# A transformer block on one core: loads by need and own orders in the opening, and the causal mask by blocks of 32

## The chip, the core and the metric

The kernel runs on one core of a Trainium2 chip. The metric is the device time of one execution in microseconds. A core has a matrix engine (TensorE, PE in the profile; its weight loads are PEld), VectorE (DVE), ScalarE (ACT), GpSimd (POOL) and SyncE (SP), which here only issues DMAs. They run side by side and wait for each other by semaphores.

## The reference

16 sequences of 256 tokens, width 256. Attention with an adapter ahead of it, then a conditional layer and a gated FFN, each with a residual:

```python
h = relu(x @ W1[lang] + b1); u = x + h @ W2[lang] + b2     # adapter by language
n = layernorm(u) * gamma[lang] + beta[lang]
q = (n @ Wq.T) as 16 heads of 16; k = n @ Wk.T; v = n @ Wv.T   # one key/value head
mask = (q_pos >= k_pos)                                    # 256 tokens: the window of 256 hides nothing
probs = softmax(where(mask, q k / 4, -1e30)); x = x + (probs v) @ Wf.T + bf
y = gelu(x @ fc1.T + b); y = [y @ fc2.T + b | y @ experts[id].T + b]
h = silu(y w1) * (y w2); h = gelu(h h1); h = gelu(h h2)    # each with its scales
x = x + (h w3) * s3
```

The whole runs in float32; the big products are taken as sums of fp32r parts.

## The kernel before

The program is written by hand for each engine, with the instructions of an engine in the order of its code. There is no scheduler: every order that matters is written out in the functions `iteration` of each engine, in `all_iterations`, and in the straight code ahead of it.

Attention works in a pipeline over the 16 batches. Iteration b does four things at once: the front of batch b + 2 (adapter, normalisation, projections of queries and keys), the maxima of batch b + 1, the scores and exponentials of batch b, and the tail of batch b - 1 (probabilities times values, output projection, residual). Iteration -1 and iteration 0 (which have no tail, and -1 no scores) stand ahead of a hardware loop over iterations 1 to 12, and 13 to 15 behind it.

Queries and keys of a batch lie in one of three slots of `q_t` and `keys`. A slot of 64 rows per parity of heads holds the high and low parts of 16 query channels (rows 0 to 47) and two rows for the negated maximum (48 and 49); rows 50 to 63 were zero. SP moves the queries into the slot with six DMAs (`move_queries`, L321), and the maxima with four (`move_maxima`, L330).

The maxima of a batch take 12 units. `max_scores` (L1282, L1285) computes the scores of two or four heads for one tile of 128 queries into one of two banks, 512 columns of float32 in all, and adds the causal mask to the 128x128 diagonal blocks by a bf16 matmul of the identity with a mask of -1e30: 512 columns in the four units of the first query tile, 256 in the eight of the second. VectorE takes the maxima (L927), splits them (L941, L943), TensorE transposes them (L1290), ScalarE copies them out. `scores` (L1301) then computes the scores with the maximum subtracted, ScalarE the exponentials (L624), and GpSimd sets what lies above the diagonal to zero (L521).

In the opening SP issues all constant loads one after another and GpSimd clears `q_t` and the values; TensorE runs nine matmuls on zeros (L1484, `keep_warm`) while the first loads are under way. `load_front` loads the input and adapter of a batch in five DMAs: three that wait for the adapter matmuls of the batch ahead (`load_inputs`, L293 to L295) and two that wait for its normalisation (`load_rest`, L301, L302). After the moves of batch 2, SP loads the first two chunks of the hidden layers' weights (L414, L415) and copies the FFN weights from their input tensor to a scratch tensor in memory in one DMA (L338); `load_ffn` loads them from there at the end of the loop. TensorE's seven constant loads are counted by `const_loaded` (7 x 16 = 112), for which its transposes, ScalarE's first query copy and GpSimd's cast of the identity (L506) wait; the reciprocal root of the variance (L512) is GpSimd's as well, behind that cast.

## Time and profile before

| | us |
|---|---|
| median of 3 runs (1142.23 to 1147.89) | 1143.06 |
| the profiled execution | 1147.46 |
| its span | 1145.7 |
| TensorE busy (96%) | 1103.2 |
| VectorE busy (68%) | 783.1 |
| ScalarE busy (51%) | 589.5 |
| GpSimd busy (15%) | 173.4 |

### The profile page before, as it was taken

What the parts mean: (1) busy time and instruction counts of PE and PEld (TensorE: products, weight loads), DVE (VectorE), ACT (ScalarE), POOL (GpSimd) and SP (SyncE); (2) the same over time, 40 slices, a digit from 0 to 9 for tenths busy, and PEclk for the clock granted to TensorE, in tenths of its full rate; (3) what the DMA queues carried; (4) which work ended last, traced back from release to release, by engine and by line L of the source; (5) the groups of instructions that cost most, each with busy time, mean ns of one, the idle gap of its engine ahead of it and who ended that gap; (6) DMA issues with size and microseconds to landing.
All of it is one profiled execution on the core that took longest, in us unless ns stands there. A gap on an engine that the chain in (4) does not pass through costs nothing.

```text
span 1145.7 us, 17992 instructions
## 1 busy us (share of the span) xinstructions
PE 1103.2 (96%) x5947; PEld 869.3 (76%) x5963; DVE 783.1 (68%) x1377; ACT 589.5 (51%) x990; POOL 173.4 (15%) x192
## 2 busy tenths in 40 slices
PE   5697999999998999999999999999999999999998
PEld 3465777676765888888888888888888888888886
DVE  2565777777776567566487775777757787568875
ACT  1154656565656445434365654656545564455653
POOL 2021222222245443541000000000000000000000
PEclk9688999999999999999999999999999999999999
DMA  4455555546474456545414443144430444404421
GB/s 134 68 150 171 106 101 101 100 101 103 99 205 148 166 200 210 214 174 185 155 41 164 165 147 110 37 165 147 164 111 11 164 142 162 144 0 147 147 92 38
DMA packets 80591, 148.57 MB, mean 130 GB/s; under 512 B 15328, under 2 KB 41840, under 8 KB 80368
## 3 DMA queue, kind: packets, MB, share of 16 engines
q1 hardware_dynamic: 71026, 126.92, 38.8%
q10 hardware_dynamic: 9518, 21.11, 5.2%
q8 instruction: 19, 0.31, 0.1%
q14 instruction: 28, 0.23, 0.1%
HBM read 107.63 MB, written 30.41 MB: 120 GB/s over the span
## 4 chain that ended last, share of the span: by engine, by line
PE 91%; DVE 3%; DMA 1%; ACT 1%; SPq 1%; issue 1%; ACTq 0%; POOL 0%; DVEq 0%; POOLq 0%
PE bank L1599 35%; PE bank L1561 10%; PE bank L1364 7%; PE bank L1611 5%; PE bank L1282 4%; PE bank L1537 4%; PE bank L1531 4%; PE bank L1301 3%; PE bank L1248 3%; PE bank L1320 2%; PE bank L1356 2%; PE bank L1285 2%; PE bank L1218 2%; DMA vec<-in_cond_vec 1%; PE bank L1228 1%; PE bank L1258 1%
## 5 line engine op out<-in xcount | busy, mean ns | idle before, releaser
L1599 PE MATMUL bank<-op_hi,w_ring 128*128 128x512 f32 x896 | 348.7, 389 | 0.0
L1599 PE MATMUL bank<-op_lo,w_ring 128*128 128x512 f32 x896 | 348.6, 389 | 0.0
L1118 DVE TENSOR_TENSOR op_lo<-x_blk,op_hi 128x512 fp32r<-128x512 f32 x288 | 193.4, 683 | 30.4 <-ACT op_hi L805 30.3
L805 ACT ACTIVATE op_hi<-x_blk 128x512 fp32r<-128x512 f32 x288 | 162.8, 620 | 73.5 <-PE bank L1599 69.3
L1599 PEld LDWEIGHTS bank<-op_lo,w_ring 128*128 128x128 f32 x896 | 168.2, 188 | 35.0
L1599 PEld LDWEIGHTS bank<-op_hi,w_ring 128*128 128x128 f32 x896 | 168.1, 188 | 35.0
L927 DVE TENSOR_REDUCE neg_max<-bank 128x2 f32<-128x512 f32 (+1 forms) x192 | 124.8, 684 | 35.7 <-PE bank L1285 34.4
L624 ACT ACTIVATE p<-bank 128x512 f32<-128x512 f32 x192 | 108.7, 596 | 39.0 <-PE bank L1301 34.7
L829 ACT ACTIVATE x_blk<-x_blk,scales 128x512 f32<-128x512 f32 x96 | 69.3, 722 | 67.0 <-DVE x_blk L1171 28.9
L1561 PE MATMUL bank<-tile_hi,ffn_w 128*128 128x512 f32 x256 | 101.6, 397 | 0.0
L1561 PE MATMUL bank<-tile_lo,ffn_w 128*128 128x512 f32 x256 | 100.9, 394 | 0.0
L521 POOL TENSOR_SCALAR_AFFINE_SELECT p<-p 128x512 f32<-128x512 f32 (+1 forms) x96 | 75.9, 791 | 162.6 <-ACT p L624 162.5
L1301 PE MATMUL bank<-q_t,keys 128*128 128x512 f32 x192 | 94.0, 505 | 0.6 <-ACT p L624 0.6
L757 ACT ACTIVATE g_raw<-bank,fc_bias 128x512 f32<-128x512 f32 x64 | 44.0, 689 | 91.8 <-PE bank L1364 77.6
L1282 PE MATMUL bank<-keys,q_t 128*128 128x256 f32 (+1 forms) x256 | 85.9, 392 | 2.6 <-DVE neg_max L927 2.5
L817 ACT ACTIVATE sil<-bank,scales 128x512 f32<-128x512 f32 x64 | 43.9, 688 | 79.2 <-PE bank L1561 79.1
L1126 DVE SCALAR_TENSOR_TENSOR x_blk<-bank,scales,sil 128x512 f32<-128x512 f32 x64 | 48.1, 751 | 51.9 <-PE bank L1561 49.8
L1282 PEld LDWEIGHTS bank<-keys,q_t 128*128 128x128 f32 x256 | 49.7, 199 | 11.1 <-DVE neg_max L927 5.5
L562 POOL TENSOR_TENSOR comb<-comb 128x512 f32<-128x512 f32 x32 | 49.5, 1546 | 56.5 <-DVE g_parts L1084 55.0
L1561 PEld LDWEIGHTS bank<-tile_hi,ffn_w 128*128 128x128 f32 x256 | 48.1, 188 | 11.9
L1561 PEld LDWEIGHTS bank<-tile_lo,ffn_w 128*128 128x128 f32 x256 | 48.2, 188 | 11.2
L1285 PE MATMUL bank<-mask,ident_b 128*128 128x256 bf16 (+1 forms) x176 | 56.6, 322 | 0.0
(126 smaller groups left out, 1741.4 us busy)
## 6 DMA issues: line engine op xcount, KB each, us to landing
w_ring<-hid_scratch SPq DMA_DIRECT2D x112, 512.0 KB, 4.6
hid_scratch<-comb ACTq DMA_DIRECT2D x8, 1792.0 KB, 7.8
q_t<-q_high SPq DMA_DIRECT2D x64, 128.0 KB, 4.9
comb<-in_hid_d ACTq DMA_DIRECT2D x6, 768.0 KB, 5.1
xt<-in_x_t SPq DMA_DIRECT2D x16, 256.0 KB
xtok<-in_x_tok SPq DMA_DIRECT2D x16, 256.0 KB
resid<-in_x_t SPq DMA_DIRECT2D x16, 256.0 KB, 3.0
q_t<-q_rest SPq DMA_DIRECT2D x32, 128.0 KB, 4.6
```

The source lines that it names most:

```text
L521: nc.gpsimd.affine_select(out=v, in_=v, compare_op=ALU.is_ge, fill=0.0, base=0, pattern=[[0, v.shape[1]], [1, P]], channel_multiplier=-1). ...
L624: nc.scalar.activation(dst.rearrange("p c t -> p (c t)"), score_bank[par][:, :], ACT.Exp).then_inc(s["exp_done"], 1)
L805: nc.scalar.activation(op_hi[:, o % OP_RING, k], x_blk[:, operand_home(o), k], ACT.Copy).then_inc(s["op_hi"], 1)
L829: nc.scalar.activation(x_blk[:, at[block], m], src, ACT.Gelu, scale=sc[:, KB * row + m:KB * row + m + 1]).then_inc(s[made], 1)
L927: nc.vector.tensor_reduce(neg_max[:, t, first:first + pairs, :].rearrange("p c a -> p (c a)"), max_bank[u % 2][:, :].rearrange("p (c k) -> ...
L1118: nc.vector.tensor_tensor(op_lo[:, o % OP_RING, k], x_blk[:, operand_home(o), k], op_hi[:, o % OP_RING, k].bitcast(F32), ALU.subtract).the ...
L1282: mm(dst[:, 2 * c * seen:2 * (c + 1) * seen].rearrange("p (a k) -> p a k", a=2), q_t[slot][:, first + c, t * P:(t + 1) * P], keys[slot][:, ...
L1285: mm(diag, ident_b[:, :], mask[:, 0:2 * pairs, :], start=False, stop=True).then_inc(s["max_mm"], 1)
L1301: mm(score_bank[par][:, :].rearrange("p (c t) -> p c t", c=pairs), keys[slot][:, par, k0:k0 + P], q_t[slot][:, first:first + pairs, q0:T], ...
L1364: last = mm(bank, w[:, k, cols], v[:, k, :], start=i == 0, stop=i == len(passes) - 1)
L1561: last = mm(bank, w_at(at, k, HID, m), read(v[:, half, k, :]), start=k == 0 and v is yc_hi, stop=k == KD - 1 and v is yc_lo)
L1599: last = mm(banks[first_bank + m][:, :], w, read(v[:, q % OP_RING, k, :]), start=k == 0 and v is op_hi and i not in (P2, P3), stop=k == KB ...
```

## The change

There are two parts.

The causal mask. A table `rank_d` of 7 rows is loaded, rounded, and moved once into rows 50 to 56 of all three slots: for r = 1 to 7 the query row is 1 where the query's block of 32 is lower than r, and the key row is -1e30 where the key's block is r. Every product of queries and keys so carries the mask between blocks of 32. What is left is the triangle inside the blocks on the diagonal, and for it the mask matmul becomes four, each with 32 columns of the identity, for 32 query rows and their own 32 keys. ScalarE and VectorE write only rows 0 to 49 of the keys' slots now, and GpSimd clears the keys' slots as well.

The opening. The first adapter matmul waits for the input and the first adapter weight alone (`first_loaded`); the other constants are issued after these have landed, and wf only after the adapter inputs of batch 1. TensorE runs 10 matmuls on zeros at the start, 12 after the adapter of batch 0 and 12 after that of batch 1. Iterations -1 and 0 have orders of their own on PE, ACT and DVE. The first chunks of the hidden weights are loaded in iterations 10 and 11, and the copy of the FFN weights is cut into 12 pieces, one at the end of each loop iteration.

```diff
-WARM_LOADS, WARM_NORM = 9, 14
+WARM_LOADS, WARM_NORM, WARM_SECOND = 10, 12, 12
@@ sync
+            def move_ranks(slot):
+                sp.wait_ge(s["rank_made"], 1)
+                rows = slice(MASK_ROW, MASK_ROW + RANKS)
+                for to, part, count in ((q_t, 0, NP), (keys, 1, 2)):
+                    sp.dma_start(to[slot][rows, :, :].bitcast(F32),
+                                 rank[:, part, :].rearrange("p (c t) -> p c t", c=1).broadcast_to([RANKS, count, T])).then_inc(s["ranks_moved"], 16)
...
-            def store_ffn():
-                sp.dma_start(ffn_scratch[:, :], ffn_d).then_inc(s["ffn_copied"], 16)
+            def copy_ffn(i):
+                cols = bass.ds(i * FFN_PIECE, FFN_PIECE)
+                sp.dma_start(ffn_scratch[:, cols], ffn_d[:, cols]).then_inc(s["ffn_copied"], 16)
 
             def load_ffn():
-                sp.wait_ge(s["ffn_copied"], 16)
+                sp.wait_ge(s["ffn_copied"], 16 * FFN_PIECES)
...
-            sp.dma_start(wf[:, :, :], w_f).then_inc(s["const_loaded"], 16)
...
+            load_inputs(1, l)
+            sp.dma_start(wf[:, :, :], w_f).then_inc(s["const_loaded"], 16)
...
+            load_rest(1, l)
+            load_resid(0)
+            sp.wait_ge(s["const_made"], 7 + 2 * SLOTS)
+            for slot in range(SLOTS):
+                move_ranks(slot)
             move_queries(0, 0)
...
-            for c in range(2):
-                sp.dma_start(comb[c][:, A11:A11 + 3, :], hid_d[c, :, 0:3, :]).then_inc(comb_loaded[c % 2], 16)
-                sp.dma_start(comb[c][:, A21, :], hid_d[c, :, 3, :]).then_inc(comb_loaded[c % 2], 16)
-            store_ffn()
...
+                load_resid(b)
+                copy_ffn(b - 1)
...
+            for b in range(B - 3 - SLOTS, B - 3):
+                iteration(b, b % SLOTS)
+                if b < B - 4:
+                    load_first_chunk(b - (B - 3 - SLOTS))
@@ gpsimd: the clears of keys[0], keys[1], keys[2] beside those of q_t
+            nc.gpsimd.memset(keys[0][:, :, :].bitcast(F32), 0.0).then_inc(s["const_made"], 1)
@@ scalar
-                    nc.scalar.activation(keys[slot][:, par, :], kv[:, :], ACT.Identity,
+                    rows = slice(SLOT * par, SLOT * par + MASK_ROW)
+                    nc.scalar.activation(keys[slot][rows, par, :], kv[rows, :], ACT.Identity,
...
-            act.wait_ge(s["front_loaded"], 80)
+            act.wait_ge(s["front_loaded"], 48)
@@ vector
+            dve.wait_ge(s["rank_loaded"], 16)
+            nc.vector.tensor_copy(rank.bitcast(F32R), rank_raw).then_inc(s["rank_made"], 1)
@@ tensor
-                pe.wait_ge(s["front_loaded"], 80 * (n + 1))
+                if is_first(n):
+                    pe.wait_ge(s["first_loaded"], 32)
+                else:
+                    pe.wait_ge(s["front_loaded"], 80 * n + 48)
...
-                mm(diag, ident_b[:, :], mask[:, 0:2 * pairs, :], start=False, stop=True).then_inc(s["max_mm"], 1)
+                for at in range(0, P, BLOCK):
+                    own = slice(at, at + BLOCK)
+                    last = mm(diag[own, :, own], ident_b[:, own], mask[:, 0:2 * pairs, own], start=False, stop=True)
+                last.then_inc(s["max_mm"], 1)
```

On TensorE, in the loop, at the first two maximum units of an iteration (`bank<-keys,q_t` are the products of queries and keys, `bank<-mask,ident_b` the mask). Before:

```order
L1322 MATMUL bank<-p,values 32x128 x4
L1272 REGISTER_ALU
L1275 ISA [waits keys_out,q_moved]
L1282 MATMUL bank<-keys,q_t 128x256 [waits max_out]
L1282 MATMUL bank<-keys,q_t 128x256
L1285 MATMUL bank<-mask,ident_b 128x512
L1282 MATMUL bank<-keys,q_t 128x256 [waits max_t_out]
L1282 MATMUL bank<-keys,q_t 128x256
L1285 MATMUL bank<-mask,ident_b 128x512
L1329 REGISTER_ALU
L1340 MATMUL bank<-ident,pv 128x128 [waits hidden_out,late_out,early_out]
L1340 MATMUL bank<-ident,pv 128x128 x3
```

And now:

```order
L1415 MATMUL bank<-p,values 32x128 x4
L1360 REGISTER_ALU
L1365 ISA [waits keys_out,q_moved]
L1372 MATMUL bank<-keys,q_t 128x256 [waits max_out]
L1372 MATMUL bank<-keys,q_t 128x256
L1377 MATMUL bank<-mask,ident_b 32x4x32 x4
L1372 MATMUL bank<-keys,q_t 128x256 [waits max_t_out]
L1372 MATMUL bank<-keys,q_t 128x256
L1377 MATMUL bank<-mask,ident_b 32x4x32 x4
L1422 REGISTER_ALU
L1433 MATMUL bank<-ident,pv 128x128 [waits hidden_out,late_out,early_out]
L1433 MATMUL bank<-ident,pv 128x128 x3
```

Where one mask matmul of 512 columns stood there are four of 4 x 32 columns that write 32 rows each; the rest of the row is the same.

On TensorE in iteration -1, from the adapter of batch 1 (`bank<-xt,w1c`) on. Before:

```order
L1218 MATMUL bank<-xt,w1c 128x256
L1228 MATMUL bank<-w2c,h_t 128x256 [waits u_out,hidden_out]
L1228 MATMUL bank<-w2c,h_t 128x256
L1237 MATMUL bank<-ident,norm 128x128 [waits norm_ready]
L1237 MATMUL bank<-ident,norm 128x128 x3
L1248 MATMUL bank<-norm_t,wq 128x256 [waits q_low,norm_t_out]
L1248 MATMUL bank<-norm_t,wq 128x256 x3
L1282 MATMUL bank<-keys,q_t 128x256 [waits keys_out,q_moved]
L1282 MATMUL bank<-keys,q_t 128x256
L1285 MATMUL bank<-mask,ident_b 128x512
L1282 MATMUL bank<-keys,q_t 128x256 x2
L1285 MATMUL bank<-mask,ident_b 128x512
```

And now:

```order
L1304 MATMUL bank<-xt,w1c 128x256
L1316 MATMUL bank<-w2c,h_t 128x256 [waits u_out,hidden_out]
L1316 MATMUL bank<-w2c,h_t 128x256
L1293 MATMUL bank<-att 128x512 x12
L1325 MATMUL bank<-ident,norm 128x128 [waits norm_ready]
L1325 MATMUL bank<-ident,norm 128x128 x3
L1372 MATMUL bank<-keys,q_t 128x256 [waits ranks_moved,keys_out,q_moved]
L1372 MATMUL bank<-keys,q_t 128x256
L1377 MATMUL bank<-mask,ident_b 32x4x32 x4
L1372 MATMUL bank<-keys,q_t 128x256 x2
L1377 MATMUL bank<-mask,ident_b 32x4x32 x4
L1336 MATMUL bank<-norm_t,wq 128x256 [waits q_low,norm_t_out]
```

Twelve matmuls on zeros came in, and the first two maximum units of batch 0 stand ahead of the query projection of batch 1 (`bank<-norm_t,wq`) instead of behind it. They wait for the moves of the ranks too.

On SP in the opening, from the load of the key projection wkv on. Before:

```order
L393 DMA wkv<-in_w_kv 128x256
L394 DMA wf<-in_w_f 128x512
L395 DMA bf<-in_b_f 128x2
L396 DMA mask<-in_mask_d 128x512
L397 DMA key_row<-in_key_row_d 128x4
L312 DMA resid<-in_x_t 128x2x256
L400 DMA fc_raw<-in_fc_w 128x1024 x2
L401 DMA fc_bias<-in_fc_b 128x8
L402 DMA scales<-in_ffn_s 128x34
L289 TENSOR_LOAD in_lang_ptr
L289 REGISTER_ALU
L289 TENSOR_LOAD in_lang
```

And now (the register and load rows between are the read of a language id):

```order
L413 DMA mask<-in_mask_d 128x512
L414 DMA key_row<-in_key_row_d 128x4
L415 DMA x<-in_rank_d 7x512
L416 DMA bf<-in_b_f 128x2
L301 DMA xt<-in_x_t 128x2x256 [waits adapted_mm]
L302 ISA
L302 DMA w1c<-in_cond_w 128x2x64
L303 ISA
L303 DMA w2c<-in_cond_w 65x256
L418 DMA wf<-in_w_f 128x512
```

wf stood right behind wkv and now stands behind the three loads of batch 1 that wait for the adapter, and the load of the ranks (`x<-in_rank_d`) came in.

## Rows read from the trace of the kernel before

**Rows 1.** Busy time by stretch (start:end, length, engines, PEclk, DMA share).

```profile
core 0: us, PE busy (x) PEld busy (x) DVE busy (x) ACT busy (x) POOL busy (x), PEclk, DMA share, GB/s
...
76.33:105.36 29.03, 21.84 (x156) 14.95 (x153) 14.44 (x33) 11.77 (x23) 5.42 (x7) 0.83 0.79 252
...
184.37:204.07 19.70, 19.59 (x156) 13.98 (x153) 14.45 (x33) 11.77 (x23) 5.41 (x7) 1.00 0.55 105
...
342.00:361.00 19.00, 16.23 (x157) 10.59 (x150) 17.05 (x27) 11.76 (x19) 10.54 (x11) 1.00 0.26 74
```

**Rows 2.** TensorE in time order, a steady iteration (start, us, line, tiles).

```profile
188.58 0.39 PE L1282 MATMUL bank<-keys,q_t 128*128 128x256 f32 x2
...
189.27 0.60 PE L1340 MATMUL bank<-ident,pv 128*128 128x128 f32 x4
...
191.32 0.39 PE L1282 MATMUL bank<-keys,q_t 128*128 128x512 f32 x1
...
191.90 0.40 PE L1282 MATMUL bank<-keys,q_t 128*128 128x512 f32 x1
```

**Rows 3.** TensorE in time order, 128*32 groups of the same iteration.

```profile
184.04 0.40 PE L1322 MATMUL bank<-p,values 128*32 128x128 f32 x8
184.37 1.13 PE L1228 MATMUL bank<-w2c,h_t 65*128 65x256 f32 x4
185.43 0.42 PE L1320 MATMUL bank<-p,values 128*32 128x256 f32 x4
```

**Rows 4.** TensorE in time order, the one-column matmul at 544 us.

```profile
542.99 0.61 PE L1364 MATMUL bank<-tile_lo,fc_hi 128*128 128x512 f32 x2
543.44 0.61 PE L1364 MATMUL bank<-tile_hi,fc_lo 128*128 128x512 f32 x2
543.98 0.19 PE L1525 MATMUL bank<-ones,low_bits 128*1 128x1 f32 x2
544.10 0.74 PE L1531 MATMUL bank<-g_parts,fc2a_hi 128*128 128x512 f32 x2
544.67 0.39 PE L1531 MATMUL bank<-g_parts,fc2a_lo 128*128 128x512 f32 x1
```

**Rows 5.** TensorE in time order, the transposes of the maxima.

```profile
200.36 0.38 PE L1264 MATMUL bank<-ident,kv 128*128 128x128 f32 x2
200.60 0.40 PE L1290 MATMUL bank<-ident,m 128*32 128x128 f32 x2
200.75 0.71 PE L1301 MATMUL bank<-q_t,keys 128*128 128x512 f32 x2
```

**Rows 6.** All engines in time order, opening (DMA rows are issues).

```profile
9.83 0.29 POOL L506 CAST ident_b<-ident 128x128 bf16<-128x128 f32 x1 [2.17 <-DMA key_row<-in_key_row_d]
...
14.32 0.56 SPq L293 DMA_DIRECT2D xt<-in_x_t  x1
...
18.18 1.09 PE L1237 MATMUL bank<-ident,norm 128*128 128x128 f32 x4 [3.89 <-DVE norm L900]
...
25.52 1.31 SPq L321 DMA_DIRECT2D q_t<-q_high  x2
...
38.63 1.87 PE L1282 MATMUL bank<-keys,q_t 128*128 128x256 f32 x4
...
52.52 0.61 PE L1290 MATMUL bank<-ident,m 128*32 128x128 f32 x2 [1.23 <-DVE m L943]
...
58.67 0.99 PE L1301 MATMUL bank<-q_t,keys 128*128 128x512 f32 x1
```

**Rows 7.** DMA issues of the first 20 us (KB, us to landing).

```profile
wf<-in_w_f SPq DMA_DIRECT2D x1, 256.0 KB, 4.2
```

**Rows 8.** TensorE in time order, start and stall of iteration 1.

```profile
73.94 1.02 PE L1218 MATMUL bank<-xt,w1c 128*128 128x256 f32 x4
...
100.64 1.22 PE L1218 MATMUL bank<-xt,w1c 128*128 128x256 f32 x2 [7.18 <-DMA vec<-in_cond_vec]
```

**Rows 9.** DMA issues from 79.5 to 81 us (KB, us to landing).

```profile
ffn_scratch<-in_ffn_d SPq DMA_DIRECT2D x1, 17.3
```

More of the change, by code:

```diff
@@ L27 @@
 SLOTS = 3
+BLOCK = 32
+RANKS = T // BLOCK - 1
+MASK_ROW = MAX_ROW + 2
 V_ROWS = ((MAX_ROW + 2, 14), (SLOT + MAX_ROW + 2, 2))
@@ L82 @@
 PIECE = FFN_COLS // W_PIECES
+FFN_PIECES = B - 4
+FFN_PIECE = FFN_COLS // FFN_PIECES
 TWO_PAD = 1
[L85 removed]
+WARM_LOADS, WARM_NORM, WARM_SECOND = 10, 12, 12
 FIRST_BANKS = (4, 5, 6, 7, 4, 5, 0, 1)
@@ L650, in iteration @@
                     maxima_out(b + 1)
+                    return
+                if not tail:
+                    hidden(b + 2)
+                    exponential(b, 0)
+                    exponential(b, 1)
+                    exponential(b, 2)
+                    affine(b + 2)
+                    exponential(b, 3)
+                    exponential(b, 4)
+                    queries_high(b + 2)
+                    exponential(b, 5)
+                    exponential(b, 6)
+                    keys_copied(b + 2)
+                    exponential(b, 7)
+                    exponential(b, 8)
+                    keys_high(b + 2, (slot + 2) % SLOTS)
+                    exponential(b, 9)
+                    exponential(b, 10)
+                    maxima_out(b + 1)
+                    exponential(b, 11)
                     return
@@ L904, in keys_low @@
                 dve.wait_ge(s["keys_hi"], 2 * (n + 1))
-                for par, rows in enumerate((slice(32, 64), slice(96, 128))):
+                for par, rows in enumerate((slice(32, MASK_ROW), slice(SLOT + 32, SLOT + MASK_ROW))):
                     nc.vector.tensor_tensor(keys[slot][rows, par, :], kv[rows, :], keys[slot][rows, par, :].bitcast(F32),
@@ L1209, in _, with keep_warm @@
             mm = nc.tensor.matmul
+            def keep_warm(n):
+                for _ in range(n):
+                    mm(score_bank[0][:, :], warm[:, 1, 0:P], warm[:, 0, :], start=True, stop=True)
             def adapter_in(n, tail):
-                pe.wait_ge(s["front_loaded"], 80 * (n + 1))
-                if not is_first(n):
+                if is_first(n):
+                    pe.wait_ge(s["first_loaded"], 32)
+                else:
+                    pe.wait_ge(s["front_loaded"], 80 * n + 48)
                     pe.wait_ge(s["norm_t_out"], n)
@@ L1222, in adapter_out @@
                 pe.wait_ge(s["hidden_out"], n + 1)
-                if not is_first(n):
+                if is_first(n):
+                    pe.wait_ge(s["front_loaded"], 48)
+                else:
                     pe.wait_ge(s["u_out"], n)
@@ L1479, in iteration @@
                     scores(b, slot, 11)
-            def keep_warm(n):
-                for _ in range(n):
-                    mm(score_bank[0][:, :], warm[:, 1, 0:P], warm[:, 0, :], start=True, stop=True)
             pe.wait_ge(s["warm_made"], 1)
@@ L1694 @@
     a["key_row_d"] = key_row
+    block, r = np.arange(T) // BLOCK, np.arange(1, RANKS + 1)[:, None]
+    a["rank_d"] = np.stack([np.where(block < r, 1.0, 0.0), np.where(block == r, -1e30, 0.0)], 1).astype(np.float32)
     a["fc1_w"] = tiles(g["L0_cond2_fc1_w"].T)
```

133 lines of the change are left out of this document (99 added, 34 removed).

## The prediction

> **What bounds the kernel now.** I read the busy time by stretch first, then TensorE in time order in one repeated iteration, then the opening. In a steady iteration of the attention loop (184.37 to 204.07 us) TensorE is busy 19.59 of 19.70 us at granted clock 1.00, VectorE 14.45 and ScalarE 11.77 [rows 1]. So there TensorE's instruction stream is the time: what it gains or loses per iteration comes out of the period one for one. The iteration that starts at 76.33 does the same work (21.84 busy, the same 156 matmul records) in 29.03 us, with the DMA share at 0.79 and the clock at 0.83 [rows 1]. In the opening nothing is full; there the order of waits decides. What follows attention is not touched.
>
> **The mask in the loop.** Each of the 12 maximum units of a batch ends in one 128-column-wide mask matmul: 512 columns in four units, 256 in eight. They become four matmuls of 32 stationary columns each, 128 or 64 columns long, on four column quarters. By length alone this is a gain. What the old one costs: from 188.58 to 189.27 run two matmuls of 256 columns, the 512-column mask and a score matmul of 512, 0.69 us; at clock 1.00 (the 2.4 GHz level) 512 columns are 0.213 us, so the mask costs 0.69 - 0.43 = 0.26. From 191.32 to 191.90, 0.58 us, with two matmuls of 512 beside the 256-column mask: 0.15 [rows 2]. Sum 4 x 0.26 + 8 x 0.15 = 2.2 us an iteration.
>
> The new one changes the shape of the array twice per unit, from 128\*128 to 128\*32 and back. The trace has such a detour around almost no work: at 543.98 a one-column matmul between 512-column ones. Two of these take 0.45 us (542.99 to 543.44), so six take 1.35; but from 542.99 to 544.67, with six and the detour in between, pass 1.68 us. The detour costs 0.33 us for one column [rows 4]: 0.09 before it, 0.12 in it and after it, and 0.12 more because the next weight load was not made ahead (two matmuls from 544.10 take 0.57 instead of 0.45). The loop's own 128\*32 groups show the same going out: the last eight recorded matmuls of 128 columns, two passes on four quarters, take 0.33 us from 184.04 to 184.37 where 0.11 each would be 0.22, and the four passes of 256 columns that follow take 1.06 from 184.37 to 185.43 instead of 0.86, the next detour's entry included [rows 3]. That eight fit into two passes says that the four quarters do run side by side.
>
> Against it stands one case: the transposes of the maxima are 128\*32 too, and from 200.36 to 200.75 there is no such gap; the pair at 200.60 takes 0.15 us [rows 5]. These are transposes, and the new mask matmuls are plain ones, as at 543.98 and in the groups; so I take the detour. The Trainium skill (TensorEngine Tiling, Key Properties) says that changing the tiling mode drains the engine; by that rule the sum is the one made here. The same page's table of theoretical speedup promises up to four times for a free dimension of 32 or less; by that alone the masks would fall to a quarter. The rows side with the first.
>
> New price of a unit: 0.33, plus 0.02 for three more starts, plus the stream of 128 (0.05) or 64 columns (0.03): 0.40 and 0.38. Sum 4 x 0.40 + 8 x 0.38 = 4.6, less 2.2: +2.35 us per iteration. Bounds: without any detour, at the 0.15 us for two passes of the transposes, a unit costs at most 0.10, so -1.0 per iteration; with the quarters one after another +3.45. Nothing hides it while TensorE is at 19.59 of 19.70. It counts in full in the twelve loop iterations and the one after them (13 x 2.35 = 30.6); in the next, where TensorE is busy 16.23 of 19.00 us [rows 1], half (1.2). The two batches of the opening have VectorE's maxima beside them and are inside the estimate below. Together +31.8.
>
> The key and query rows that carry the block mask lie in rows that were zero; the matmuls over them keep their size, so they cost only their moves at the start. The narrower row ranges on ScalarE and VectorE keep their column counts: nothing.
>
> **The copy of the FFN weights.** Before, SP queues 2 MB of hidden weights and then one copy inside memory, 17.3 us from issue to landing [rows 9]; the loads and moves behind it wait, and TensorE stands 7.18 us before 100.64 for the vector load [rows 8], after which the clock is low. Against a steady period it costs 29.03 - 19.70 = 9.3 us [rows 1]. After, a twelfth goes out at the end of each iteration (17.3 / 12 = 1.4 us of queue time) and the hidden chunks in the tenth and eleventh. What is late next: each piece is behind the moves of the maxima on SP and ahead of loads that have most of an iteration; the last piece must land before the load of the FFN weights, and that load is wanted only after attention. I cost this at nothing and take -9.3. At worst a chunk of 1 MB gives 2 back.
>
> **The opening.** The first adapter matmul waits for two loads instead of five, so the end of the two adapter steps (14.32 [rows 6], when SP goes on) comes about 3 us earlier. But what follows gives it back. On GpSimd the reciprocal root of batch 0 stands behind the cast of the identity, and that behind seven constant loads; the last of them, wf, is now issued after three loads of batch 1, which wait for the adapter. With the adapter done at about 11.0 and SP there at 11.3, three issues (2.0), wf's 4.2 to landing [rows 7], cast and root (0.3 + 0.7) and the normalisation (0.8) give 19.3 for the transposes that started at 18.18 [rows 6]: 1 us late. On SP six moves of ranks at 0.65 us (1.31 for two [rows 6]) are then ahead of batch 0's queries: these go out near 26.6 instead of 25.52.
>
> The gain comes after that. The maximum units of batch 0 started at 38.63 behind batch 1's query projection; now they are ahead of it and start when the queries are there, at about 34.7 (26.6, six issues of 0.65, and 4.2 to landing as for wf), and the split of fc1 no longer stands before batch 1's statistics. The stretch from there to the transposes of the maxima took 13.9 us (52.52); at that length they come 4 us earlier, and I take 5, since TensorE is kept running ahead of it and may hold its clock. Iteration 0 took 58.67 - 52.52 = 6.2 us to its first scores and then ran to 73.94 [rows 6, 8]; its new order gives perhaps 2 more. I take iteration 1 at 67 instead of 73.94: -7. Bounds: 0, if the clock stays low and the late constants pass through, and -14, if all of it runs at the high level.
>
> **Sum.** 1147.46 us for the profiled execution, -7 - 9.3 + 31.8 = 1163. That execution lies 4.4 us above the median of the three runs, so the median goes from 1143.06 to 1158.5; I say 1158, 1.3% slower. Under 0.5%, or 5.7 us, a measurement can hardly tell from no change.
>
> **Rivals.**
> A, no detour: bf16 quarters behave like the transposes [rows 5]. For it: one case in the loop itself. Against it: three plain cases with the gap [rows 3, 4]. Then 13.5 x -1.0 = -14 with the two gains of 16: 1143 - 30 = 1113. By the skill's speedup table it would come out this way.
> B, half a detour: the load after the group is made ahead, which takes 0.12 off each unit (0.28 and 0.26, so +1.0 per iteration, +13). With -16: 1140, no change.
> C, the quarters don't overlap when they are this short. The two one-column matmuls of [rows 4] last 0.19 together, so each further start is about 0.03; 64 columns in four turns are +0.08 and 128 +0.15, 1.1 per iteration: +15, 1173.
> D, the opening is worth 14 instead of 7, or nothing: inside the forecast's own range, 1151 to 1165.
> The forecast is on the slower side, and A is the rival on the other: it decides in the very first max unit of the loop, and the sign turns where a unit costs about 0.11 us less than I say (16 / 13.5 / 12 = 0.10 above the old price).
>
> **Chances.** Forecast 0.61 (own range 1149 to 1168), A 0.17, B 0.15, C 0.07. Faster by over 0.5% (below 1137.3): A, and 0.06 of B and 0.02 of the forecast, 0.25. Within 0.5%: 0.09 of B and 0.04 of the forecast, 0.13. Slower: 0.62. The range from 1124 to 1171 leaves out A and the upper half of C.
>
> **What the profile of the changed kernel would show.** The period of the loop: 22.0 us (22.05) if I am right, 18.7 under A, 20.7 under B, 23.1 under C. The first weight load of a mask group should start some 0.09 us after the matmul ahead has streamed, and the load after it together with its matmul. No iteration should be longer than its neighbours by the 7 us wait for the vector load. Transposes of batch 0 near 19, of its maxima near 47, iteration 1 near 67. The page's share of TensorE stays, since it counts these gaps partly as busy; the period is what tells. I am wrong if the period is below 20.5, or if iteration 1 begins before 60 or after 74.

## The result, and the profile after

The changed kernel takes 1166.8 us in the median (1164.8 to 1167.2), the kernel before 1143.4 on the same chip: ratio 1.0197, 95% interval 1.017 to 1.0223. Slower by 2.0%, on the forecast's side and inside its range (1124 to 1171), but 8.8 us above the 1158 that it named. The profiled execution of after took 1164.8 us, its span 1163.2; before's span was 1145.7.

Where the 17.5 us between the two spans lie, by the starts of the second adapter matmul of each iteration:

| stretch | before | after | difference |
|---|---|---|---|
| start to iteration 1 | 76.33 | 77.83 | +1.5 |
| iteration 1 | 29.03 | 21.59 | -7.4 |
| iterations 2 to 12 (11 periods) | 217.04 | 237.54 | +20.5 |
| iteration 13 to the end | 823.3 | 826.2 | +2.9 |

The busy time by stretch of the changed kernel, the first loop iteration, a steady one and the one that starts at 336.96:

```profile
core 0: us, PE busy (x) PEld busy (x) DVE busy (x) ACT busy (x) POOL busy (x), PEclk, DMA share, GB/s
77.83:99.42 21.59, 21.43 (x192) 14.47 (x188) 14.77 (x33) 11.86 (x23) 5.43 (x7) 1.00 0.43 80
207.38:228.95 21.57, 21.43 (x192) 14.45 (x189) 14.77 (x33) 11.86 (x23) 5.42 (x7) 1.00 0.50 105
336.96:358.00 21.04, 20.44 (x188) 13.92 (x184) 15.68 (x34) 11.52 (x23) 9.04 (x10) 1.00 0.77 239
```

A steady iteration now takes 21.57 to 21.60 us where it took 19.70 [rows 1]. TensorE is busy 21.43 of 21.57: it still sets the time. Iteration 1 has no stall of its own any more. On the page the share of TensorE is 97%, as before (96%). Part of the mask's price stands in the row of its weight loads, as idle time that nothing released ("issue"): 52.6 us, where the same row of before has 34.0:

```profile
L1377 PEld LDWEIGHTS bank<-mask,ident_b 128*32 128x32 bf16 x768 | 19.7, 93 | 52.6 <-issue 44.5
```

TensorE in time order, a unit whose mask is four matmuls of 128 columns and one with four of 64, in the same iteration (start, duration, line, tiles):

```profile
213.32 0.40 PE L1372 MATMUL bank<-keys,q_t 128*128 128x256 f32 x2
213.64 0.24 PE L1377 MATMUL bank<-mask,ident_b 128*32 128x128 bf16 x4
213.81 0.50 PE L1394 MATMUL bank<-q_t,keys 128*128 128x512 f32 x1
214.15 0.60 PE L1325 MATMUL bank<-ident,norm 128*128 128x128 f32 x4
...
214.82 0.39 PE L1372 MATMUL bank<-keys,q_t 128*128 128x512 f32 x1
215.14 0.21 PE L1377 MATMUL bank<-mask,ident_b 128*32 128x64 bf16 x4
215.28 0.49 PE L1394 MATMUL bank<-q_t,keys 128*128 128x512 f32 x1
215.61 0.40 PE L1372 MATMUL bank<-keys,q_t 128*128 128x512 f32 x1
```

From 213.32 to 214.15 run two products of 256 columns, the mask group and one score matmul of 512 columns: 0.83 us, of which 0.43 are the streams of the products at 512 columns per 0.213 us. So the group costs 0.40. From 214.82 to 215.61, with two products of 512 columns: 0.79 - 0.43 = 0.36. In the second unit the product streams from 214.82 until 215.03, the mask starts at 215.14 (0.11 later), the next matmul at 215.28 (0.14, of which 0.03 are the stream), and the one behind it at 215.61, 0.33 later instead of 0.21 (0.12). That is the detour of [rows 4] with its three parts: a wait going out, one coming back, and a weight load that isn't made ahead.

The opening (all engines; SPq rows are issues of DMAs):

```profile
15.26 0.29 POOL L543 CAST ident_b<-ident 128x128 bf16<-128x128 f32 x1 [6.20 <-DMA wf<-in_w_f]
...
17.22 1.09 PE L1325 MATMUL bank<-ident,norm 128*128 128x128 f32 x4 [6.10 <-DVE norm L958]
...
21.03 0.99 SPq L327 DMA_DIRECT2D q_t<-att_t  x1
...
26.30 1.28 SPq L337 DMA_DIRECT2D q_t<-q_high  x2
...
34.63 0.79 PE L1372 MATMUL bank<-keys,q_t 128*128 128x256 f32 x2 [2.90 <-DMA q_t<-q_high]
```

```profile
48.71 0.39 PE L1383 MATMUL bank<-ident,m 128*32 128x128 f32 x2 [1.24 <-DVE m L1001]
...
54.24 1.22 PE L1394 MATMUL bank<-q_t,keys 128*128 128x512 f32 x2 [1.56 <-DMA q_t<-m_t]
...
73.71 1.91 PE L1304 MATMUL bank<-xt,w1c 128*128 128x256 f32 x4 [3.87 <-DMA vec<-in_cond_vec]
```

The cast of the identity stood 6.20 us for wf, the transposes followed at 17.22 (18.18 before [rows 6]), six moves of ranks went from 21.03 until the queries' moves at 26.30, and the maximum units started at 34.63 (38.63 before). The maxima were transposed 3.8 us and the first scores started 4.4 us earlier than before. Then iteration 0 gave it back: 54.24 to 73.71 is 19.5 us, where before took 15.3 [rows 6, 8], and the last 3.87 us of it are a wait for the vector load.

### The profile page after: what moved, and what is told of

Read it like the earlier page. It is cut to its first block, busy times and chain, and to the rows that moved or that the text cites. A ratio compares the mean times of both kernels' runs of the same rounds, so it can differ in the third digit from the quotient of the medians.

```text
span 1163.2 us, 19240 instructions
## 1 busy us (share of the span) xinstructions
PE 1128.9 (97%) x6563; PEld 875.0 (75%) x6564; DVE 788.5 (68%) x1378; ACT 591.7 (51%) x990; POOL 175.0 (15%) x195
## 4 chain that ended last, share of the span: by engine, by line
PE 92%; DVE 2%; SPq 1%; issue 1%; ACT 1%; DMA 1%; POOL 1%; DVEq 0%; POOLq 0%; ACTq 0%
PE bank L1722 35%; PE bank L1684 10%; PE bank L1457 7%; PE bank L1734 5%; PE bank L1372 5%; PE bank L1394 5%; PE bank L1660 4%; PE bank L1654 4%; PE bank L1336 3%; PE bank L1449 2%; PE bank L1413 2%; PE bank L1377 2%; PE bank L1304 1%; PE bank L1433 1%; PE bank L1346 1%
## 5 line engine op out<-in xcount | busy, mean ns | idle before, releaser
L985 DVE TENSOR_REDUCE neg_max<-bank 128x2 f32<-128x512 f32 (+1 forms) x192 | 129.1, 688 | 55.3 <-PE bank L1377 51.5
L887 ACT ACTIVATE x_blk<-x_blk,scales 128x512 f32<-128x512 f32 x96 | 69.3, 722 | 67.0 <-DVE x_blk L1250 28.9
L1377 PEld LDWEIGHTS bank<-mask,ident_b 128*32 128x32 bf16 x768 | 19.7, 93 | 52.6 <-issue 44.5
L1372 PEld LDWEIGHTS bank<-keys,q_t 128*128 128x128 f32 x256 | 47.1, 194 | 11.4 <-DMA q_t<-q_high 3.1
```

Source lines behind the costliest of these rows:

```text
L887: nc.scalar.activation(x_blk[:, at[block], m], src, ACT.Gelu, scale=sc[:, KB * row + m:KB * row + m + 1]).then_inc(s[made], 1)
L985: nc.vector.tensor_reduce(neg_max[:, t, first:first + pairs, :].rearrange("p c a -> p (c a)"), max_bank[u % 2][:, :].rearrange("p (c k) -> ...
L1372: mm(dst[:, 2 * c * seen:2 * (c + 1) * seen].rearrange("p (a k) -> p a k", a=2), q_t[slot][:, first + c, t * P:(t + 1) * P], keys[slot][:, ...
```

## The experiments

All twelve ran in three sets, each beside runs of the kernel before (median 1146.0, 1146.6 and 1146.6 us on those chips, 1143.4 beside the changed kernel). Kernels of different sets are best compared by these ratios; differences in us below are between profiled executions or between medians.

### The parts apart

**The mask undone.**

```diff
-                for at in range(0, P, BLOCK):
-                    own = slice(at, at + BLOCK)
-                    last = mm(diag[own, :, own], ident_b[:, own], mask[:, 0:2 * pairs, own], ...)
+                mm(diag, ident_b[:, :], mask[:, 0:2 * pairs, :], start=False, stop=True)
```

> The changed kernel with one thing undone: the mask is again one matmul of the whole identity (the ranks stay in the keys and queries, so blocks above the diagonal are masked twice). My theory: of the change only the four-quarter groups cost time in the loop, 1.88 us an iteration by the periods (21.59 against 19.71). Then the period is 19.7 again, 12 iterations give back 22.6 and the iterations behind them about 2, so 1166.8 - 25 = 1142 us, and iteration 1 takes 19.7 as well. Rival: part of the longer period comes from the pieces of the FFN copy or the narrower key writes; then the period stays at 20.2 or more and the time at 1150 or more.

1137.15 us (1135.9 to 1140.76), ratio 0.9935 (0.9914 to 0.9955). The steady iteration, and the same two kinds of unit as above:

```profile
211.82:231.56 19.74, 19.63 (x157) 13.98 (x153) 14.44 (x33) 11.86 (x23) 5.43 (x7) 1.00 0.59 112
```

```profile
217.41 0.40 PE L1372 MATMUL bank<-keys,q_t 128*128 128x256 f32 x2
...
218.12 0.60 PE L1325 MATMUL bank<-ident,norm 128*128 128x128 f32 x4
...
218.79 0.40 PE L1372 MATMUL bank<-keys,q_t 128*128 128x512 f32 x1
...
219.38 0.40 PE L1372 MATMUL bank<-keys,q_t 128*128 128x512 f32 x1
```

Period 19.74, so the rival (20.2 or more) falls. The two units take 0.71 and 0.59 us where the four quarters took 0.83 and 0.79: 0.12 and 0.20 more, 4 x 0.12 + 8 x 0.20 = 2.1 an iteration; 1.87 of it come through, since behind some units the next instruction is late in either kernel. The old mask is a bf16 matmul as well and takes only 0.07 and 0.05 us over its stream (0.28 and 0.16 against 0.21 and 0.11), so the type isn't what costs. The span is 28.9 us shorter than the changed kernel's (1134.3): 4.0 before iteration 1 (73.79), 22.5 in twelve periods, 2.4 behind.

**The quarters alone**, in the kernel before.

```diff
-                mm(diag, ident_b[:, :], mask[:, 0:2 * pairs, :], start=False, stop=True)
+                for at in range(0, P, 32):
+                    own = slice(at, at + 32)
+                    last = mm(diag[own, :, own], ident_b[:, own], mask[:, 0:2 * pairs, own], ...)
```

> The kernel before with the four-quarter mask groups alone (no ranks: what lies between blocks of 32 above the diagonal is not masked for the maxima). Theory: the period goes from 19.7 to 21.6, and with the iterations behind the loop the time is 1143.4 + 25 = 1168; the 7.4 us stall of iteration 1 stays. Rival: the stall, which waits for a transfer, swallows part of the longer stream and the opening of before hides the rest, so that less than 20 us is added.

1169.67 us (1169.06 to 1169.91), ratio 1.0209 (1.0188 to 1.0231): 24 us more. Iteration 1 and a steady one:

```profile
76.70:103.84 27.14, 23.66 (x193) 15.45 (x189) 14.78 (x33) 11.78 (x23) 5.43 (x7) 0.89 0.82 269
212.19:233.76 21.57, 21.43 (x192) 14.46 (x188) 14.77 (x33) 11.78 (x23) 5.43 (x7) 1.00 0.47 93
```

The period is 21.57 again: the mask alone makes it, without the ranks. Iteration 1 takes 27.14, where 29.03 + 1.9 was expected: the longer stream lies partly beside the wait for the transfer, and the granted clock is 0.89 there instead of 0.83 [rows 1]. The rival (less than 20 us added) falls, but the stall of before does hide some of the mask's price. Iteration 1 starts at 76.70 us, against 76.33 in before.

**The copy in pieces alone**, in the kernel before.

```diff
-            for c in range(2): ...        # both hidden chunks
-            store_ffn()
+            ...                           # at the end of each loop iteration: copy_ffn(b - 1)
+            ...                           # behind iterations 10 and 11: load_first_chunk(0), (1)
```

> The kernel before with the FFN copy cut into 12 pieces and the first hidden chunks in iterations 10 and 11, nothing else. Theory: iteration 1 takes 19.7 us instead of 29.03, and nothing comes up elsewhere: -9.3, so 1134 us. Rival 1: the gain is smaller because in the changed kernel part of it was the opening's, 1139. Rival 2: the pieces delay moves and loads of the loop or the load of the FFN weights at its end, and the time stays at 1143.

1139.06 us (1135.1 to 1142.73), ratio 0.9944 (0.9925 to 0.9963): -6.4 us (4 to 9), between the theory and rival 1. Iteration 1 and a steady one:

```profile
73.11:92.86 19.75, 19.63 (x157) 13.96 (x153) 14.44 (x33) 11.78 (x23) 5.43 (x7) 1.00 0.47 87
211.18:230.89 19.71, 19.61 (x156) 13.96 (x152) 14.45 (x33) 11.78 (x23) 5.43 (x7) 1.00 0.59 112
```

Iteration 1 is as short as any, which is the whole 9.3. The edit moves the hidden chunks as well as the copy; which of the two made the stall isn't separated. Elsewhere the profiles differ by a few us both ways: iteration 1 starts at 73.11 where before, with the same opening, had 76.33, and from iteration 13 to the end this execution is 2.1 us longer. An opening so differs by 3 us from one execution to the next. This kernel also prices the new opening: it has the old one and a ratio of 0.9944, the kernel with the mask undone has the new one and 0.9935 (iteration 1 at 73.79). As changed, and without the new mask, the opening was worth 1 us by the ratios and 1.9 by the medians, within some 3.

### The mask's price

**No mask matmul at all.** The products alone, the last one closing the bank.

```diff
-                for at in range(0, P, BLOCK): ...
+                    last = mm(..., keys[slot][:, :, 0:seen], start=c == 0, stop=c == pairs - 1)
```

> The changed kernel without any mask matmul: the triangle inside the blocks of 32 on the diagonal is not masked for the maxima (the exponentials above the diagonal are still set to zero later). This gives the full price of each mask. If TensorE's stream sets the period and the old mask costs 0.26 and 0.15 us a unit, the period is 19.7 - 2.2 = 17.5 us, the four-quarter groups then cost 21.6 - 17.5 = 4.1 us an iteration (0.34 a unit, against the 0.38 to 0.40 I had said), and the time is 1142 - 13.5 x 2.2 = 1112. Rival: without the mask something else bounds (VectorE, 14.4 us of maxima and splits, or the banks that it frees), the period stays above 18.5 and the time above 1125.

1128.58 us (1126.97 to 1132.63), ratio 0.9847 (0.9825 to 0.9868). The steady iteration:

```profile
209.41:228.36 18.95, 18.64 (x145) 13.43 (x141) 14.02 (x33) 11.75 (x23) 5.59 (x7) 1.00 0.62 117
```

The rival was right: the period is 18.94, not 17.5. The old mask's matmuls stream for 2.2 us, but leaving them out gives 0.8; TensorE is busy 18.64 of 18.95 us, and in between it now waits for VectorE and ScalarE. One such place, two units followed by the transposes of `pv`, for which ScalarE's copy of `pv` has to be done (212.05 + 0.60):

```profile
211.91 0.74 PE L1372 MATMUL bank<-keys,q_t 128*128 128x256 f32 x4
212.74 0.63 PE L1429 MATMUL bank<-ident,pv 128*128 128x128 f32 x4
```

From start to start pass 0.83 us, where four streams of 256 columns need 0.43; with the mask undone the same stretch takes 1.04, so leaving out two masks that stream for 0.43 gave 0.21. In this order of instructions even a mask for nothing could have brought only 0.8 us an iteration, and rival A's forecast (-1.0) lay beyond the floor.

**The same detours, twice the matmuls.**

```diff
-                for at in range(0, P, BLOCK):
+                for i, at in enumerate(2 * list(range(0, P, BLOCK))):
-                    ... start=False, stop=True)
+                    ... start=False, stop=i >= P // BLOCK)
```

> The changed kernel with eight mask matmuls in each group instead of four: the same four quarters a second time, so the mask is added twice. The array's shape changes as often as before. Theory (the detour is the price, not its matmuls): a second round costs only its stream, 128 or 64 columns (0.05 or 0.03 us), and 0.01 for the starts: 4 x 0.06 + 8 x 0.04 = +0.56 us an iteration, period 22.15, time +7 us. Rival (each short matmul has its price): the period before went up by 1.88 us against a mask whose stream was 2.2, so 48 matmuls would cost up to 4.1 us, 0.085 each; 48 more then add 4.1, period 25.7, time +54 us.

1172.74 us (1171.08 to 1174.41), ratio 1.0242 (1.0201 to 1.0283). The steady iteration:

```profile
210.04:232.09 22.05, 21.90 (x240) 14.68 (x236) 14.83 (x33) 11.85 (x23) 5.43 (x7) 1.00 0.51 103
```

48 matmuls more cost 0.47 us, 0.01 each (22.05 against the forecast's 22.15). The rival (4.1 us) falls: the number of short matmuls isn't the price.

**Half the detours, the same matmuls.**

```diff
+                if u % 2 == 0:
+                    return
+                for bank in max_bank:
+                    ...                   # four quarters in each of the two banks
```

> The changed kernel with the masks of two units put together: an even unit issues its products only, the odd one behind it its products and then the eight mask matmuls of both banks. Six detours an iteration instead of twelve, with the same matmuls. Theory: a group costs about 0.36 us, of which 0.05 are its streams, so six detours fewer give 6 x 0.31 = -1.9 us an iteration: period 19.7, time 1166.8 - 13 x 1.9 = 1142. Rival: VectorE gets the even unit's bank later and frees it later, and TensorE then stands for it; without any mask the period was 18.94 where the streams alone promised 17.5, so such waits lie close behind. Then the period is 20.5 or more and the time 1152 or more.

1164.67 us (1163.88 to 1165.67), ratio 1.0173 (1.0143 to 1.0202). The steady iteration, and in it a pair that gains and two that lose:

```profile
208.26:229.38 21.12, 20.67 (x193) 14.16 (x189) 14.27 (x33) 11.87 (x23) 5.54 (x7) 1.00 0.52 107
```

```profile
216.12 0.24 PE L1380 MATMUL bank<-mask,ident_b 128*32 128x64 bf16 x8
216.38 1.99 PE L1336 MATMUL bank<-norm_t,wq 128*128 128x256 f32 x8
...
220.60 0.40 PE L1397 MATMUL bank<-q_t,keys 128*128 128x512 f32 x1
221.20 0.49 PE L1372 MATMUL bank<-keys,q_t 128*128 128x512 f32 x1 [0.20 <-DVE neg_max L985]
...
222.64 1.10 PE L1372 MATMUL bank<-keys,q_t 128*128 128x512 f32 x2
223.67 0.24 PE L1380 MATMUL bank<-mask,ident_b 128*32 128x64 bf16 x8
223.84 0.70 PE L1452 MATMUL bank<-att_t,wf 128*128 128x256 f32 x2
```

Only 0.47 us an iteration, a quarter of the theory's 1.9; the rival was right. The group itself does what it should: eight mask matmuls take 0.17 us to the next matmul, from 223.67 to 223.84 (0.26 in the first pair, at 216.12), and one way out and back serves them, where a group of four took 0.14 and had a way of its own. But the product at 221.20 starts 0.60 after the matmul at 220.60 (0.21 would do) and waits for VectorE, and the two from 222.64 to 223.67 take 1.03 instead of the 0.53 that two streams and the way out need. VectorE gets both banks of a pair at once and gives the first back late. In this iteration TensorE's weight loads wait for the maxima in four places, 1.55 us together, and in the changed kernel's in none; with two banks for the maxima, pairing takes back most of what it gives.

**Another shape**: two halves of 64 columns.

```diff
-                for at in range(0, P, BLOCK):
-                    own = slice(at, at + BLOCK)
+                for at in range(0, P, 2 * BLOCK):
+                    own = slice(at, at + 2 * BLOCK)
```

> The changed kernel with each mask group cut in two halves of 64 columns of the identity instead of four quarters of 32 (64 query rows and their own 64 keys, streams of 256 or 128 columns). Theory: any change of the array's shape costs the same detour, so only the streams grow, by 0.05 or 0.03 us a unit: period 21.6 + 0.45 = 22.05 us, time 1171. Rival: only the narrow shape costs, or two starts are cheaper than four: period 21.3 or less.

1174.61 us (1170.2 to 1179.02, two runs), ratio 1.0249 (1.0195 to 1.0303). The steady iteration:

```profile
208.76:230.87 22.11, 21.98 (x169) 14.55 (x165) 14.83 (x33) 11.85 (x23) 5.41 (x7) 1.00 0.50 102
```

22.11 against 22.05 foretold: 128\*64 costs the same detour and streams longer. Two matmuls are no cheaper than four, and the rival (21.3 or less) falls.

### The opening

**The late loads first.**

```diff
             load_inputs(3, l)
-            move_queries(2, 2)
             load_rest(3, l)
+            move_queries(2, 2)
```

> The changed kernel with one order changed on SP in the opening: the two loads of batch 3 that wait for the normalisation of batch 2 go out before the move of batch 2's queries instead of behind it. In the changed kernel TensorE stood 3.87 us for the vector load before iteration 1 (73.71). Theory: that wait goes and nothing else is late, so iteration 1's adapter starts at 69.8 us, the clock doesn't fall there, and the time is 4 to 5 us shorter: 1162. Rival: the moves of batch 2's queries now stand behind the wait for the normalisation, or VectorE's last maxima end the iteration instead: iteration 1 not before 72.5, less than 1.5 us gained.

1161.39 us (1160.56 to 1162.03), ratio 1.0143 (1.0114 to 1.0173). SP (issues) and TensorE:

```profile
61.89 0.34 SPq L310 DMA_DIRECT2D vec<-in_cond_vec  x1
```

```profile
71.39 1.12 PE L1304 MATMUL bank<-xt,w1c 128*128 128x256 f32 x4
```

The vector load goes out at 61.89, ahead of the queries' moves (65.86); in the changed kernel it was behind the queries' moves at 64.14 to 68.0. The wait is gone, the adapter follows the last scores at once at 71.39, the second adapter matmul is at 73.88 instead of 77.83, the span 3.8 us shorter, the median 5.4. The clock behind it stayed at 1.00. The theory's size holds, its time of 69.8 doesn't (71.39): this execution was 1.5 us late before iteration 0 began (50.48 against 48.94).

**The opening mended**: this edit, wf at the front, no ranks, the old mask.

```diff
             sp.dma_start(wkv[:, :, :], w_kv).then_inc(s["const_loaded"], 16)
+            sp.dma_start(wf[:, :, :], w_f).then_inc(s["const_loaded"], 16)
...
             load_inputs(1, l)
-            sp.dma_start(wf[:, :, :], w_f).then_inc(s["const_loaded"], 16)
...
-            for slot in range(SLOTS):
-                move_ranks(slot)
```

> The changed kernel with the mask as one matmul again (its own comparison is the kernel with the mask undone: 1137.15 us, second adapter matmul of iteration 1 at 73.79), and three more edits in the opening: no ranks are loaded, rounded or moved; wf is issued with wq and wkv, so GpSimd's cast of the identity doesn't wait for it; the two late loads of batch 3 go out before the move of batch 2's queries. Theory: the normalisation of batch 0 comes 2 us earlier and its queries leave at about 21.5 us instead of 26.3, the maximum units of batch 0 start near 30 instead of 34.6, and the wait of 4 us before iteration 1 goes: iteration 1 at about 65, time 1129. Rival: what is won early is given back where VectorE's maxima and the moves follow each other and where the clock falls when TensorE idles: iteration 1 at 70 or later, time 1134 or more.

1122.89 us (1120.94 to 1123.67), ratio 0.9809 (0.9781 to 0.9837): faster than both kernels. All engines:

```profile
12.20 0.29 POOL L540 CAST ident_b<-ident 128x128 bf16<-128x128 f32 x1 [3.13 <-DMA bf<-in_b_f]
...
14.15 0.63 PE L1320 MATMUL bank<-ident,norm 128*128 128x128 f32 x4 [2.38 <-DVE norm L955]
...
15.89 1.99 PE L1331 MATMUL bank<-norm_t,wq 128*128 128x256 f32 x8 [1.11 <-ACT norm_t L631]
...
19.38 1.29 SPq L337 DMA_DIRECT2D q_t<-q_high  x2
...
28.02 0.50 PE L1365 MATMUL bank<-keys,q_t 128*128 128x256 f32 x2 [1.43 <-DMA q_t<-q_high]
```

```profile
56.48 1.13 PE L1299 MATMUL bank<-xt,w1c 128*128 128x256 f32 x4
```

Iteration 1's first adapter matmul starts at 56.48; its second, by which the stretches of the other runs are cut, at 58.97 against 73.79 with the mask undone alone: 14.8 earlier, where about 9 were forecast. The median is 14.3 below the kernel with the mask undone, where 8 were forecast; the rival (1134 or more) falls. And TensorE's query projection takes 1.99 us where it took 3.60 to 3.78: the clock was never low. Over the whole span it stands at 1.00. What I had bounded at -14 is there, once three things are out of its way. The next two runs put wf and the ranks back, one at a time, and the third takes out the matmuls on zeros. The late loads were not put back in this kernel.

**wf late again**: the edit with wf undone in that kernel.

```diff
-            sp.dma_start(wf[:, :, :], w_f).then_inc(s["const_loaded"], 16)   # behind wkv
+            sp.dma_start(wf[:, :, :], w_f).then_inc(s["const_loaded"], 16)   # behind load_inputs(1)
```

> The kernel with the opening mended (1122.9 us, iteration 1's adapter at 56.48) with one edit taken back: wf is again issued behind the three loads of batch 1 that wait for the adapter, so GpSimd's cast of the identity waits for it. Theory: the transposes of batch 0 come at 17.4 us instead of 14.15, the clock falls while TensorE waits (it was low from 15.9 to 22.7 in the changed kernel), the query projection takes 3.8 us instead of 2.0, and the queries leave at 24 us instead of 19.4: iteration 1 comes 5 us later and the time is 1128. Rival: the lost 3 us are hidden later, because the maximum units of batch 0 are bound by VectorE: less than 2 us, 1125 or less.

1128.14 us (1127.04 to 1129.53), ratio 0.9848 (0.9824 to 0.9871): +5.2, as expected (the rival said 2 or less). All engines:

```profile
15.22 0.29 POOL L540 CAST ident_b<-ident 128x128 bf16<-128x128 f32 x1 [6.15 <-DMA wf<-in_w_f]
...
19.37 3.78 PE L1331 MATMUL bank<-norm_t,wq 128*128 128x256 f32 x8 [1.11 <-ACT norm_t L631]
```

The cast waits 6.15 us for wf, and the query projection behind it starts at 19.37 (15.89 before) and takes 3.78. Iteration 1's second adapter matmul is at 64.20 instead of 58.97.

**The ranks kept.**

```diff
+            for slot in range(SLOTS):
+                move_ranks(slot)          # and their load, the rounding on VectorE, the wait
```

> The kernel with the opening mended (1122.9 us), but with the ranks loaded, rounded on VectorE and moved by SP into the three slots ahead of batch 0's queries, as in the changed kernel; the mask stays one matmul. Theory: SP issues the six moves from about 17.5 us on and takes 5.2 us for them (21.03 to 26.2 in the changed kernel), so the queries leave at 22.7 instead of 19.38, TensorE waits 3 us longer before the maximum units of batch 0 and its clock falls there: iteration 1 at 60 to 62, time 1127 to 1129. Rival: the moves lie beside GpSimd's and VectorE's work and cost under 1.5 us: 1124 or less.

1130.18 us (1127.96 to 1131.17), ratio 0.9857 (0.9831 to 0.9883): +7.3, above the 4 to 6 expected. All engines:

```profile
11.85 0.41 DVE L1131 CAST att_t<-x 7x512 fp32r<-7x512 f32 x1 [9.72 <-DMA x<-in_rank_d]
...
14.33 0.71 POOL L549 TENSOR_TENSOR rstd<-veps,half 128x2 f32<-128x2 f32 x1 [1.88 <-DVE veps L953]
...
24.95 1.28 SPq L337 DMA_DIRECT2D q_t<-q_high  x2
```

The six moves end when the queries' moves start, at 24.95 instead of 19.38. What I had not seen is the rounding at 11.85: it stands on VectorE ahead of batch 0's statistics and waits for the ranks' load, so GpSimd's root comes at 14.33 instead of 12.53. Iteration 1's second adapter matmul is at 68.63, 9.7 late. The granted clock was 0.56 from 16 to 23 us and again from 33 to 40, where the mended kernel had 1.00. This is the price of the block mask that the loop doesn't show.

**Without the fillers** after the two adapters.

```diff
-            keep_warm(WARM_NORM)
-                    keep_warm(WARM_SECOND)
```

> The kernel with the opening mended (1122.9 us, granted clock 1.00 over the span) without the 12 matmuls on zeros after the adapter of batch 0 and the 12 after that of batch 1; the 10 at the start stay. Theory: the clock stays high in that kernel because TensorE's waits are short or filled. Without the fillers it stands for 5 us at 9 us and for 4 us at 22 us, the clock falls for one or two stretches of about 7 us as in the changed kernel, and the time is 4 to 8 us longer: 1127 to 1131. Rival: the fillers do nothing, since what follows waits for DMAs and VectorE: 1123, within 1 us.

1126.59 us (1125.46 to 1130.98), ratio 0.9843 (0.9813 to 0.9873): +3.7, just short of the 4 to 8 expected. The busy time by stretch, first with the fillers, then without:

```profile
9.00:16.00 7.00, 3.50 (x18) 1.60 (x17) 2.60 (x8) 1.02 (x2) 1.06 (x4) 1.00 0.55 150
16.00:22.00 6.00, 4.97 (x22) 3.71 (x23) 1.78 (x5) 2.64 (x5) 0.00 (x0) 1.00 0.71 230
```

```profile
9.00:14.00 5.00, 0.27 (x2) 0.23 (x2) 2.60 (x8) 0.00 (x0) 1.07 (x4) 0.62 0.47 118
14.00:21.00 7.00, 5.89 (x16) 4.21 (x15) 0.50 (x1) 1.62 (x3) 0.00 (x0) 0.54 0.70 225
```

With them TensorE is busy 3.50 of 7.00 us from 9 on and the granted clock is 1.00 in the next stretch (the 2.4 GHz level); without them it is busy 0.27 of 5.00 us, and the clock is 0.62 and 0.54, mostly at the lower level. So the query projection that follows takes 3.78 us instead of 1.99.

## Why the prediction was right, and where not

**The bound.** Right for what is added: TensorE's stream sets the loop before and after, and of the 2.1 us more in an iteration 1.87 came out. Not so for what is taken away: without any mask 2.2 us of its stream went and 0.8 came out, so "one for one" holds in one direction only.

**The mask.** The mechanism was right, the size too high. A unit costs 0.40 and 0.36 us by its rows (I had 0.40 and 0.38), the old one 0.28 and 0.16 (I had 0.26 and 0.15); with 0.12 and 0.20 a unit and the rest hidden by waits that were there anyway, the period rose by 1.88 instead of 2.35. That the detour is the price is shown from two sides: twice the matmuls in the same detours cost 0.47 us an iteration, not 4.1, and another shape costs the same. Behind the opening the mask costs 24.9 us of span (22.5 in twelve periods, 2.4 after them), where the sum had 31.8. Another 4.0 lie in the two batches of the opening, which I had counted inside the opening's own term. Rivals B and C needed a period of 20.7 and 23.1, A 18.7: none came. I chose the plain matmul at 544 us as the model over the transposes of the maxima, and that choice carried the sign. By the rule of the Trainium skill (TensorEngine Tiling, Key Properties) a change of the tiling mode drains the engine; all five kernels with such groups agree, at 0.11 to 0.12 us on the way out. Of the up to four times in its table of theoretical speedup nothing came for groups that are entered and left again: here four times as many matmuls, each a quarter as long, took longer.

**The copy.** The stall went as costed: iteration 1 from 29.03 to 19.75 us. Against the medians the whole edit gave 6.4 us (4 to 9) instead of 9.3.

**The opening.** This term failed: -7 was said, with the mask of two batches in it. In the profiled executions iteration 1 started at 73.71 instead of 73.94 and its second adapter matmul 1.5 us later than before; without the mask's 4.0 it is -1 to -2 by the runs of the parts. Its first half held (queries at 34.63 against 34.7, maxima's transposes at 48.71 against 47.5). The step that failed is "its new order gives perhaps 2 more": I had the rows of TensorE's order in view, and not SP's, where the load of batch 3's vector had moved behind the moves of batch 2's queries. It cost 3.9 us. The rest isn't explained by it: with that load in time, iteration 0 still took 20.9 us from its adapter to iteration 1's (50.48 to 71.39), where before took 21.0, with the new mask's groups and a low stretch of the clock in it. A late wf and the ranks, which the forecast had costed for their delay alone, cost 5.2 and 7.3 us in the mended kernel, where the clock was low behind them.

**The sum.** For the profiled execution 1163 was said, and 1164.8 came. That nearness is luck: by the spans the mask behind the opening came out 7 us cheaper than in the sum and the opening 8.5 us dearer (+1.5 for -7), and the two cancel. The median misses by 8.8 because the forecast took off 4.4 us for a slow profiled execution of before, while that of the changed kernel lies 2.0 below its own median. By the ratios, where all runs count, it is the mask with about 30 for 31.8 (the opening's 4.0 in it), the copy with 3 less gained and the opening with 5 to 6 less gained.

**The chances.** The forecast, with its 0.61, came: its own range of 1149 to 1168 holds the 1166.8, near the upper end. What I had as bound D, -14 with the clock high throughout, exists, but in another kernel.

**What stays open.** Why the pieces give 6.4 us in the medians and 9.3 in their iteration, and the mask 24 us added to before but 29.7 taken from after; a few us of both may be the scatter of the openings and the stall, but the shares weren't separated. Why plain matmuls on 128\*32 pay the detour and the transposes of the maxima don't: both the forecast's choice and the runs only show that it is so. And which of the mended opening's parts keeps the clock high: a late wf, the ranks, and the matmuls on zeros left out each bring a low stretch; the late loads were tried in the changed kernel alone. The mended opening with ranks and quarters was not run; as an estimate, the parts give 1160 (1122.9 + 7.3 + 29.7), and the run with the late loads first less the price of a late wf gives 1156 (1161.4 - 5.2).

## What to carry to other kernels

Look at the shape of the array before the column count: a group of small-tile matmuls between full ones costs its way out and back, some 0.33 us here, however little it computes, so gather such groups (if the banks allow it) or leave the big matmul. Before paying for a cheaper instruction, leave it out altogether once: the floor of 18.94 says that in this order of instructions the best of all masks was worth 0.8 us an iteration. When an opening is reordered, follow the last constant, the last wait and the last queue to the instruction that needs them on every engine; one late load, six small moves and one order on the DMA queue hid 14 us.

## What the runs showed of the hardware

The quarters of one group do run side by side: four matmuls of 128 columns take 0.17 us to the next instruction (213.64 to 213.81) and four of 64 columns 0.14, 0.03 apart where four turns of 64 more columns would be 0.11. The way out of the full array costs 0.11 to 0.12 us, and the first weight load after the way back is not made ahead (0.12 to 0.13 more), for 128\*32 and 128\*64 alike. The transposes of the maxima, 128\*32 too, show none of it [rows 5].

The 24 matmuls on zeros gave 3.7 us net. Without them the transposes of batch 0 start 0.35 us earlier (13.80 against 14.15) and batch 0's first maximum unit 1.9 later (29.93 against 28.02), behind a query projection that ran at the lower clock. In the opening of the changed kernel the granted clock was low (0.50) from 15.9 until 22.7 us; it fell while TensorE stood, from 11.1 to 17.2.
